# Queries and keys projected apart and scores on two 64-row halves, in a fused decoder layer on one core

## What is computed

```python
def _L0_attn_ref(x, norm_scale, wq, wk, wv, w_out, b_out):
    h = _rmsnorm(x, norm_scale)
    q = jnp.einsum('bsd,dhe->bshe', h, wq)
    k = jnp.einsum('bsd,dhe->bshe', h, wk)
    v = jnp.einsum('bsd,dhe->bshe', h, wv)
    q = (q * head_dim ** (-0.5)).astype(softmax_dtype)
    weights = jax.nn.softmax(jnp.einsum('bqhd,bkhd->bhqk', q, kf), axis=-1)
    new_vals = jnp.einsum('bhqk,bkhd->bqhd', weights, v)
    return jnp.einsum('bqhe,hed->bqd', new_vals, w_out) + b_out

x = x + _L0_attn_ref(_layernorm(x), ...)
x = x + _L0_xattn_ref(ctx_1024, ctx_1024, _layernorm(x), ...)
x = x + _L0_ffn_ref(_layernorm(x), ...)
```

## Time and profile before

| | before |
|---|---|
| median of 3 runs (435.38 to 438.6) | 437.57 us |
| span of the profiled execution | 435.1 us |
| TensorE busy | 402.7 us, 93% |
| VectorE busy | 322.4 us, 74% |
| ScalarE busy | 262.0 us, 60% |
| GpSimd busy | 161.5 us, 37% |

### The profile page before, as it was taken

The page is one execution under the profiler, slowest core; times in us unless marked ns, Lnnn a source line. Parts: engine busy times, 40 slices in busy tenths (PEclk is TensorE's granted clock), DMA queues, the critical chain, the costliest instruction groups (busy, mean ns, idle before and its releaser), DMA issues.

```text
span 435.1 us, 9030 instructions
## 1 busy us (share of the span) xinstructions
PE 402.7 (93%) x2981; PEld 333.1 (77%) x2981; DVE 322.4 (74%) x780; ACT 262.0 (60%) x808; POOL 161.5 (37%) x177
## 2 busy tenths in 40 slices
PE   3889999999999999999999999999999999998646
PEld 3787888788878887888888887898788888866115
DVE  2677767866897489867886689748976779757883
ACT  2576665665566565575566556665566565825672
POOL 1055334542454344542454245434454244421000
PEclk9899999999999999999999999999999999999668
DMA  7400000000100010001000010001000000000003
GB/s 232 130 2 2 0 2 2 2 2 2 36 2 3 2 36 0 0 0 36 0 0 0 2 34 0 0 0 36 0 0 0 24 2 2 1 2 0 0 0 98
DMA packets 11878, 7.50 MB, mean 17 GB/s; under 512 B 1232, under 2 KB 11216, under 8 KB 11856
## 3 DMA queue, kind: packets, MB, share of 16 engines
q1 hardware_dynamic: 11568, 6.69, 5.2%
q10 hardware_dynamic: 288, 0.52, 0.4%
HBM read 6.16 MB, written 1.05 MB: 17 GB/s over the span
## 4 chain that ended last, share of the span: by engine, by line
PE 65%; DVE 18%; issue 8%; ACT 6%; DMA 1%; POOL 1%; DVEq 0%; POOLq 0%; ACTq 0%
PE o_bank L467 11%; PE pT L458 9%; PE acc_bank L474 7%; DVE negmax L897 5%; PE score L437 5%; PE score L435 5%; PE score L436 5%; ACT prob L731 4%; PE side_bank L435 3%; PE q_bank L435 2%; PE q_bank L437 2%; PE side_bank L437 2%; PE q_bank L436 2%; PE side_bank L436 2%; PE side_bank L512 2%
## 5 line engine op out<-in xcount | busy, mean ns | idle before, releaser
L1249 POOL TENSOR_TENSOR prob<-prob,rinv 128x512 f32<-128x512 f32 x128 | 133.0, 1042 | 200.6 <-DVE rinv L901 196.8
L731 ACT ACTIVATE prob<-score,negmax 128x256 f32<-128x256 f32 x256 | 118.9, 470 | 103.3 <-DVE negmax L897 103.2
L897 DVE TENSOR_REDUCE negmax<-score 128x2 f32<-128x512 f32 x128 | 87.6, 685 | 51.3 <-PE score L437 50.4
L904 DVE COPY pT<-pT 128x512 f32<-128x512 f32 x128 | 86.4, 677 | 0.0
L458 PE MATMUL pT<-ident,prob 128*128 128x128 f32 x512 | 76.6, 272 | 0.0
L435 PE MATMUL score<-ht_hi,q_hi 128*128 128x256 f32 x256 | 75.0, 293 | 0.0
L437 PE MATMUL score<-ht_hi,q_lo 128*128 128x256 f32 x256 | 72.0, 281 | 0.0
L436 PE MATMUL score<-ht_lo,q_hi 128*128 128x256 f32 x256 | 71.7, 280 | 0.0
L467 PE MATMUL o_bank<-pT,v_sb 128*64 128x256 f32 x512 | 69.4, 392 | 0.0
L458 PEld LDWEIGHTS pT<-ident,prob 128*128 128x128 f32 x512 | 58.9, 141 | 0.4 <-issue 0.4
L474 PEld LDWEIGHTS acc_bank<-wo_sb,oT 128*128 128x128 f32 x256 | 33.4, 190 | 24.3 <-issue 24.2
(11 more groups left out here) (209 smaller groups left out, 600.3 us busy)
## 6 DMA issues: line engine op xcount, KB each, us to landing
c_sb<-in_ctx_dram SPq DMA_DIRECT2D x8, 256.0 KB, 2.9
x_sb<-in_x_dram SPq DMA_DIRECT2D x8, 128.0 KB, 2.8
out_dram<-xn_all SPq DMA_DIRECT2D x4, 256.0 KB, 2.3
big<-in_L_attn_wk_dram ACTq DMA_DIRECT2D x1, 512.0 KB, 3.9
big<-in_L_attn_wq_dram SPq DMA_DIRECT2D x1, 512.0 KB, 6.1
big<-in_L_attn_wv_dram SPq DMA_DIRECT2D x1, 512.0 KB, 6.9
wo_sb<-in_L_attn_w_out_dram SPq DMA_DIRECT2D x1, 512.0 KB, 6.7
w_sb<-in_L_ffn_w_dram SPq DMA_DIRECT2D x2, 256.0 KB, 4.6
```

Of the source, the lines that this page charges most:

```text
L731: last = nc.scalar.activation(prob[:, slot, t, :], score_bank[r][:, t * S:(t + 1) * S], ACT.Exp, bias=negmax[:, slot, t:t + 1], scale=1.0, ...
L897: nc.vector.tensor_reduce(negmax[:, slot], score_bank[r][:].rearrange("p (t k) -> p t k", k=S), X_AXIS, ALU.max, negate=True).then_inc(max ...
L904: nc.vector.tensor_copy(pT[:, slot].rearrange("p k q -> p (k q)"), pT_bank[r][:]).then_inc(pT_done, 1)
L1249: nc.gpsimd.tensor_tensor(prob[:, slot], prob[:, slot], rinv[:, slot].unsqueeze(2).to_broadcast([P, QT, S]), ALU.mult).then_inc(prob_done, 1)
```

## The change

Queries and keys are projected apart, with Wq (scaled) and Wk of a pair, both heads side by side: `q_bank` holds the pair's queries in its first half and its keys in the second. A head's operands are then 64 rows deep, head r on rows 64r to 64r+63, and the score matmuls of the two heads alternate, each into its own bank. The weights' high and low parts (`wqk_hi`, `wqk_lo`) are made in SBUF from the loaded weights; the turning of Wq and Wk and the products A are gone.

The loop is reordered. On TensorE place 0 moves ahead of the scores, the scores of both heads stand together behind one wait for both heads' exps, both `turn_probs` follow, then place 1, then the output projection ahead of the values. On ScalarE place 0 moves ahead of the first head's exps and place 1 between the two heads' exps. On VectorE both maxima come first, a head's reciprocal of the step before moves to the step's start, and the statistics, aggregates and normalises move by up to a step. On GpSimd the rstd of the second norm moves from step 2 to step 1 and the bias add from step 1 to step 2.

Two quarters of V (V1, V3) are now made in the batch that uses them (W1, W3), and UX is halved into UX0 and UX1 of 128 columns each.

```diff
-PLACE = {(0, 0): "TC", (1, 1): "TH", (2, 0): "V0", (2, 1): "TX", (3, 0): "QX", (3, 1): "SX0",
-         (4, 0): "SX1", (4, 1): "PX0", (5, 0): "PX1", (5, 1): "UX", (6, 0): "OX", (6, 1): "V1",
-         (7, 0): "V2", (7, 1): "V3"}
+PLACE = {(0, 0): "TC", (0, 1): "W1", (1, 0): "W3", (1, 1): "TH", (2, 0): "V0", (2, 1): "TX", (3, 0): "QX",
+         (3, 1): "SX0", (4, 0): "SX1", (4, 1): "PX0", (5, 0): "PX1", (5, 1): "UX0", (6, 0): "UX1", (6, 1): "OX",
+         (7, 0): "V2"}
...
-            def project_q(pair, hp):
-
-                for r in range(2):
-                    a = (slice(None), pair // 4, r, pair % 4)
-                    last = three_passes(q_bank[:, r * S:(r + 1) * S], a_hi[a], a_lo[a], ht_hi[:, hp], ht_lo[:, hp])
+            def project_qk(pair, hp):
+
+                for n in range(2):
+                    last = three_passes(q_bank[:, n * S:(n + 1) * S], wqk_hi[:, n, pair, :], wqk_lo[:, n, pair, :],
+                                        ht_hi[:, hp], ht_lo[:, hp])
                 last.then_inc(q_raw, 1)
 
-            def scores(r, parity, hp):
+            def scores(parity):
 
                 for t in range(QT):
-                    q = (slice(None), parity, r, slice(t * P, (t + 1) * P))
-                    last = three_passes(score_bank[r][:, t * S:(t + 1) * S], q_hi[q], q_lo[q],
-                                        ht_hi[:, hp], ht_lo[:, hp])
-                last.then_inc(score_raw, 1)
+                    for n, (query, key) in enumerate(((q_hi, q_hi), (q_hi, q_lo), (q_lo, q_hi))):
+                        for r in range(2):
+                            rows = slice(r * E, (r + 1) * E)
+                            last = nc.tensor.matmul(score_bank[r][:, t * S:(t + 1) * S],
+                                                    query[rows, parity, 0, t * P:(t + 1) * P], key[rows, parity, 1, :],
+                                                    start=(n == 0), stop=(n == 2))
+                            if t == QT - 1 and n == 2:
+                                last.then_inc(score_raw, 1)
...
                 if more_q:
-                    project_q((j + 3) % PAIRS, parity if j < PAIRS - 3 else 1 - parity)
-                if more_scores:
-                    pe.wait_ge(exp_done, 2 * g + 3)
-                    scores(0, j % 2, hp)
-                pe.wait_ge(prob_done, 2 * g + 1)
-                wait(pe, pT_done, 2 * g - 1)
-                turn_probs(0, 2 * j % 8)
+                    project_qk((j + 3) % PAIRS, parity if j < PAIRS - 3 else 1 - parity)
                 if task := side_at(kind, j, 0):
                     side(kind, b, 1 - parity, i, task)
                 if more_scores:
                     pe.wait_ge(exp_done, 2 * g + 4)
-                    scores(1, j % 2, hp)
+                    scores(j % 2)
+                pe.wait_ge(prob_done, 2 * g + 1)
+                wait(pe, pT_done, 2 * g - 1)
+                turn_probs(0, 2 * j % 8)
                 pe.wait_ge(prob_done, 2 * g + 2)
                 wait(pe, pT_done, 2 * g)
                 turn_probs(1, 2 * j % 8 + 1)
+                if task := side_at(kind, j, 1):
+                    side(kind, b, 1 - parity, i, task)
...
             def step(kind, b, parity, i, j):
...
-            for half in range(2):
-                act.wait_ge(wT_raw, 2 * half + 2)
-                copy(wkT[:, 4 * half:4 * half + 4, :], weight_banks[2 * half + 1][:].rearrange("p (j d) -> p j d", d=P)
-                     ).then_inc(wkT_done, 1)
...
+            act.wait_ge(load_wk, 16)
+            weights_hi(1, 0)
+            act.wait_ge(load_wq, 16)
+            weights_hi(0, 0)
             act.wait_ge(load_scale, 16)
             side("start", -1, 0, "TH")
...
+                if ahead(kind, j, 1):
+                    dve.wait_ge(exp_done, 2 * g + 4)
+                    invert_sums((2 * j + 3) % 8)
...
+                if cross and j == 2:
+                    normalise(1, tiles(xn2), tiles(x1_sb), b, xn2_done)
...
-            for task in ("UX", "OX"):
+            for task in AFTER_LAST:
```

More of the change, by code:

```diff
@@ L555, in step @@
                     project_out((j - 2) % PAIRS)
[L556 to L557 removed]
+                if not (kind == "first" and j < 1):
+                    if j == 1:
+                        pe.wait_ge(side_free, side_before(kind, b))
+                    slot = 2 * (j - 1) % 4
+                    values((j - 1) % PAIRS, (slot, slot + 1), 1 - parity if j == 0 else parity)
             pe.wait_ge(consts, 1)
             side("start", -1, 0, 0, "TH")
[L562 to L579 removed]
             pe.wait_ge(side_free, 1)
[L582 to L583 removed]
+            pe.wait_ge(wqk_lo_done, 2)
+            project_qk(0, 0)
             pe.wait_ge(load_cross, 16 * 8)
@@ L602, in _ @@
             nc.tensor.matmul(pT_bank[1][:, D:2 * D], xbv_wide[:], xwoT[:], start=True, stop=True).then_inc(e_raw, 1)
-            for h in range(2):
-                pe.wait_ge(exp_done, h + 1)
-                scores(h, 1, 0)
-            side("start", -1, 0, 0, "V3")
+            pe.wait_ge(exp_done, 2)
+            scores(1)
             pe.wait_ge(e_done, 2)
             pe.wait_ge(load_wo, 16)
+            pe.wait_ge(wqk_lo_done, 4)
             over_batches(pe, step)
@@ L768, in step @@
                     split_hi((j + 3) % 2)
+                if task := side_at(kind, j, 0):
+                    side(kind, b, 1 - parity, task)
                 if more_scores:
@@ L818, in _ @@
             exps(1, 1)
+            side("start", -1, 0, "V0")
             act.wait_ge(q_raw, 3)
@@ L825, in _ @@
             exps(1, 3)
-            side("start", -1, 0, "V3")
             over_batches(act, step)
@@ L1050, in step @@
                     invert_sums((2 * j + 4) % 8)
+                if (task := side_at(kind, j, 1)) and not early:
+                    side(kind, b, 1 - parity, task)
+                if cross and j == 1:
+                    residual(b, 1 - parity)
                 if kind == "mid" and j == PAIRS - 2:
-                    aggregate(2, b, *PLAIN_NORM)
+                    dve.wait_ge(side_free, side_index(kind, b, "OX") + 1)
                 dve.wait_ge(pT_raw, 2 * g + 2)
                 keep_turned(1, 2 * j % 4 + 1)
-                if more_scores:
-                    dve.wait_ge(exp_done, 2 * g + 6)
-                    invert_sums((2 * j + 5) % 8)
                 if prepare and j == 0:
@@ L1060, in step @@
                 if cross and j == 1:
-                    residual(b, 1 - parity)
+                    aggregate(1, b, *PLAIN_NORM)
+                if kind == "mid" and j == PAIRS - 2:
+                    statistics(2, x2_of(b), b)
                 if kind == "last":
                     weights(j)
-                if task := side_at(kind, j, 1):
-                    side(kind, b, 1 - parity, task)
             dve.wait_ge(load_x[0], 16)
```

174 lines of the change are left out of this document (67 added, 107 removed).

## The result

The changed kernel takes 415.9 us (median of 4 runs, 415.53 to 416.64) against 437.1 us before (a fourth run of that kernel brought the median down from the 437.57 us of the first three): a ratio of 0.952, 95% interval 0.949 to 0.954. The profiled span went from 435.1 to 413.9 us.

A forecast was written before the change was run, and what follows sets the result against it. TensorE's own queue was taken to set the pace. The terms -18.0 - 5.5 + 1.3 + 1.4 - 4.5 + 0.5 + 1.0 gave -23.8 us, from 435.1 to 411.3 profiled, 413.8 on the median's scale; predicted 413.5, range 399 to 429.

The forecast's parts named there:

- halves, 62 steps: Score matmuls on two row halves overlap: 0.70 us saved less 0.41 for shape changes a step, -18.0 us in all.
- TH to V0: V0's wait behind TH for ht_lo, in seven batches: the reordered steps take back 5.5 of 7.0 us.
- UX halved: UX's 8 records of 256 columns become 16 of 128, in six middle batches: +1.3 us.
- V rows in the loop: V1 and V3 become W1 and W3; last batch holds two, start two fewer: +1.4 us in the loop.
- start: Setup before the loop: weight transposes and A products go, first projection near 10.3: -4.5 us (-2 to -7).
- VectorE late: VectorE's strict order at times makes a maximum late, tightest in step 2 of a batch: +1.0 us (0 to +12).
- Borders: Changes of array shape around each step's scores: 0.41 us out and back, 0.27 as bound from below.
- Rival A: Score halves do not overlap for fp32r and the shape changes come on top: 457 us, slower; chance 0.12.
- Slack of the exps: Scores wait for both heads' exps; TensorE's other work covers this with 0.25 us to spare at the thinnest.
- Rival B: Exp wait or VectorE's order sets the pace in part, 0.3 us in five of eight steps: 425 us; chance 0.18.
- Rival C: Clock falls for a tenth of the loop, about 18 us: 431 us; chance 0.08, shared with no gain at all.
- D: Larger gain: a shape change of 0.27, all of the 7.0 us back, no late maxima: 402 us; chance 0.17.

The follow-up runs named there:

- e2_full: Changed kernel with each score matmul on all 128 rows of the array instead of its own 64: 437.1 us, ratio 1.001.
- e3_extra_change: Changed kernel with head 0's four transposes of probabilities put between the scores' two halves of queries: 440.0 us, ratio 1.008.
- e6_tx_later: Changed kernel with TensorE issuing TX, the transposes of normalised x1, after the output projection and values of its step: 417.4 us, ratio 0.956.
- e5_aggregate_first: Changed kernel with VectorE's aggregation of x1's statistics ahead of the copy of head 1's turned probabilities in step 1: 412.1 us, ratio 0.942.

## Why the prediction was right, point by point

413.5 us was predicted, 415.9 measured, inside 399 to 429 and inside the likeliest case (406 to 420). Its mechanism holds: the halves overlap for fp32r, the changes of form take part of it back, TensorE's queue stays the bound. The terms:

| term | predicted | measured |
|---|---|---|
| halves, 62 steps | -18.0 | 62 x -0.35 = -21.7 |
| TH to V0 | -5.5 | -7.0 |
| UX halved | +1.3 | 6 x (1.88 - 1.54) = +2.0 |
| V rows in the loop | +1.4 | two of 0.79, +1.6 |
| start | -4.5 | -2.9 |
| end | +0.5 | +0.5 |
| VectorE late | +1.0 | 6 x 1.18 + (1.61 - 0.53) = +8.2 |

That is -19.3 of the span's -21.2; the remaining 1.9 are not resolved. In the table of groups there are effects of either sign outside the sum: the other side tasks after a change of neighbour (+0.8 a batch), and the groups of turned probabilities, 8.55 before where eight plain steps hold 8 x 0.89 = 7.12. Of these 1.4, V0's wait for ht_lo is 1.0, already counted as TH to V0; 0.4 are groups ahead of a side task.

That the total came within 2.4 us is in part luck. Three terms were forecast too favourable by 0.7, 0.2 and 1.6, a fourth by 7.2 us, and against them stood 3.7 and 1.5 us of gain more than forecast and the 1.9 not resolved. The main term was no luck: e2_full loses the whole gain with the halves' overlap, and e3_extra_change shows the border's price.

**Halves.** The pairs start in the same hundredth, as forecast. Borders measure 0.35 out and back, not 0.41: first score record 0.21 after the last projection's instead of 0.12, first pair to second 0.22 instead of 0.12, last pair to first transpose 0.21, first transposes 0.16 instead of 0.11. The bound of 0.27 (its own terms, 1.54 - 0.45 - 0.84, give 0.25) and the value 0.41 both came from the values' borders; e3_extra_change shows 0.35 for one more excursion of the scores. Since 62 steps multiply it, 0.06 us made 3.7 us. Rival A is out.

**TH to V0.** In the changed kernel TH starts at 157.88 and V0 at 160.47, right behind the projection; all of the 7.0 us came back, 1.5 more than was taken.

**The step that failed** is "late maxima +1.0": 8.2 us were measured. The prediction called step 2, with its normalise ahead of the maxima, the tightest place, and did not work it out. Counted from rows it would have been: the aggregate behind the copy of pT, 0.25 + 0.17, GpSimd 0.7, the normalise, against TX asked for directly behind the turning and no longer behind the output projection. The bound of 12 us for it was sound, the value was not. It showed not as late maxima but at TX: 2.11 us instead of 0.93 for the group ahead of it in the middle batches, 2.54 in the last one, where before TX had waited 0.53 (the output projection ahead of it took 1.08 instead of 0.55). Of the 1.18 us a batch, some 0.7 is the time for which the first normalise stood still beside GpSimd's scaling (1.05 us instead of 0.34, last section), for which the prediction had no term; this share is worked out from the rows, and no run takes it apart.

**Slack of the exps.** 0.25 at the thinnest was predicted, over 0.6 is there in a plain step; TensorE waited for exps ahead of scores for 1.84 us, once, at 24.41 in the first step. By the prediction's own count the chain from the last score's start to the exps' end took 3.0 us (39.29 to 42.26) and not 3.1, and TensorE's part to the next scores 3.6 (39.29 to 42.89) and not 3.35, since the 3.35 left out the border behind the scores (0.21). Rival B did not occur through the exps, but its second half, VectorE's strict order, is, with this hold, the 8.2 us.

**Start.** The timeline, against the earlier trace rows:

```profile
9.82 0.58 PE L430 MATMUL q_bank<-ht_hi,wqk_hi 128*128 128x256 f32 x1 [1.15 <-DVE ht_lo L931]
...
24.41 0.39 PE L447 MATMUL score<-q_hi 64*128 64x256 f32 x2 [1.84 <-ACT prob L702]
...
27.79 0.38 PE L430 MATMUL q_bank<-ht_hi,wqk_hi 128*128 128x256 f32 x1 [0.68 <-DVE q_lo L862]
```

The first projection came at 9.82, earlier than the 10.3 forecast, the second step at 27.79 instead of 26. With 1.4 for the two V rows that left, 6.8 us were there to gain, and 3.9 of them were lost, not 1.8. The rows name the waits for both heads' exps and for q_lo (1.84 and 0.68 us); the rest is not taken apart. Matmuls at half the rate stand in both kernels' starts (the six of the first projection take 1.45 us here, and the kernel before has them from 18.40 to 20.32, 0.21 apart).

**Clock.** 1.00 from 22 to 383 us, past the loop's end at 367; in the last 31 us, which the change does not touch, 0.70, against 0.72 in the last 30 us of the kernel before. Rival C is out. **D**, the larger gain, had the borders' direction right and the late maxima wrong. The forecast's last line also lost a little: its sum gives 413.8 us, and it says 413.5.

## What to carry to other kernels

Contractions of 64 on two row halves halved the time of this group, and each excursion into the 64x128 form cost 0.35 us: keep a half-array group long and whole (twelve matmuls here saved 0.70 for 0.35; six at a time, as in e3_extra_change, gave nothing, 440.0 us). Before a step is reordered for TensorE, write down for each instruction that TensorE waits for how long after the scores it is ready and what stood in between: the values' 1.0 us between scores and projection was cover for VectorE's q_lo, and moving it cost 40 us, of which an earlier q_lo brought back 10; waits for pT and oT remained. When a wait appears, shorten the chain of the engine that is late; moving the waiting instruction only passes the wait on to the next (e6_tx_later: nothing; e5_aggregate_first: 3.8 us; both with the order put right: 6.9 us).

## What the hardware showed that was not expected

TensorE does not start matmuls for two halves strictly in turn: in blocks of six the seventh started 0.11 us ahead of the fourth, 0.35 us after the first, as far as the records' lengths tell the halves apart, and blocks of three overlapped in full.

A VectorE instruction on SBUF can be held for the whole of a GpSimd instruction. The chain of waits of the changed kernel (start, us, what) splits the 1.30 us of the normalise:

```profile
163.20 0.59 issue
163.79 0.34 DVE xn L902
```

Its second half starts at 163.79, when GpSimd's scaling, 162.75 + 1.04, ends; alone the two take 0.59. It is so for all xn and veps records (both TENSOR_SCALAR) of the loop that start during a scaling: xn 0.69 to 1.05 us instead of 0.33 or 0.34, veps 0.96 or 0.97 instead of 0.17. The maxima, which read PSUM, took 0.67 to 0.69 beside a scaling as elsewhere, and the reciprocals, which are on SBUF as well, at most 0.17 either way. The order on GpSimd makes the meeting certain in step 2: this scaling is the next instruction behind rstd, so it starts 0.07 us ahead of the normalise that waits for the same rstd. Before the change, x1's normalise stood clear of it (0.34 and 0.34 in all six middle batches). The Trainium skill, "SBUF — State Buffer", in the section "SBUF: two separate sides", says that GpSimd and a VectorE instruction in a two-port mode, or with two inputs in SBUF, share a port pair which the one that starts first holds for its whole instruction. The rows of the normalise agree; in which mode it ran no view shows. The prediction had no term for this.

The first matmuls run at about half the rate: score pairs start 0.21 us apart from 14.84 to 15.69, and the matmuls of the next projection 0.12 apart from 17.06 on. The stage table of the changed kernel gives the earlier stretch a granted clock of 1.00 as well:

```profile
14.50:17.00 2.50, 2.50 (x16) 2.16 (x16) 1.55 (x3) 1.25 (x3) 0.00 (x0) 1.00 0.37 105
```

so the spacing of the records tells more there than the clock's column, which stood at 0.50 in the kernel before from 17.0 to 20.4.
